# Counting edges in shorter pieces over narrower windows, in a two-layer graph kernel

## The reference, cut to what matters

```python
e = leaky_relu(a1[src] + a2[dst]); m = segment_max(e, dst)
w = exp(e - m[dst]); alpha = w / segment_sum(w, dst)
out = segment_sum(alpha[:, :, None] * ft[src], dst)      # ft = projection of x
```

## Time and profile before

| | |
|---|---|
| median of three runs | 1255.27 us (1253.35 to 1255.71) |
| profiled execution | 1256.27 us, its span 1254.6 us |
| PE busy | 1107.9 us, 88% of the span, 8043 matmuls |
| DVE busy | 1034.4 us, 82%, 1739 instructions |
| ACT busy | 653.2 us, 52%, 1080 instructions |
| POOL busy | 159.5 us, 13% |
| DMA | 98.95 MB, mean 79 GB/s |
| mean granted clock of PE | 0.968 of full speed |

### The profile page before, as it was taken

The page is one execution under the profiler, slowest core; times in us unless marked ns, Lnnn a source line. Parts: engine busy times, 40 slices in busy tenths (PEclk is TensorE's granted clock), DMA queues, the critical chain, the costliest instruction groups (busy, mean ns, idle before and its releaser), DMA issues.

```text
span 1254.6 us, 21108 instructions
## 1 busy us (share of the span) xinstructions
PE 1107.9 (88%) x8043; PEld 921.8 (73%) x8043; DVE 1034.4 (82%) x1739; ACT 653.2 (52%) x1080; POOL 159.5 (13%) x155
## 2 busy tenths in 40 slices
PE   4787865888888888869999999999979999999996
PEld 1344454666666666659999989999968888788885
DVE  7987469999999999979488589999988765267865
ACT  0322497999999999932211046667731221223432
POOL 3000000000000000000005402111430105330111
PEclk9998876999999999989999999999989999999998
DMA  3001112202020211155403641020314112435121
GB/s 133 1 13 51 52 55 82 71 13 83 1 83 2 83 34 56 37 186 171 132 25 120 229 144 42 2 75 1 135 47 156 36 51 102 154 113 204 63 73 47
DMA packets 39859, 98.95 MB, mean 79 GB/s; under 512 B 4467, under 2 KB 17147, under 8 KB 39765
## 3 DMA queue, kind: packets, MB, share of 16 engines
q1 hardware_dynamic: 39766, 97.66, 22.8%
HBM read 70.74 MB, written 26.90 MB: 78 GB/s over the span
## 4 chain that ended last, share of the span: by engine, by line
PE 42%; DVE 36%; issue 14%; ACT 3%; DVEq 2%; DMA 1%; POOL 0%; SPq 0%; POOLq 0%; ACTq 0%
DVE R L1493 14%; PE psum L967 13%; PE psum L884 12%; PE psum L995 8%; DVE R L1623 5%; DVE R L1633 5%; DVE R L1481 4%; PE psum L784 3%; DVE LC L1356 1%; PE psum L684 1%; DVE et_lo L1650 1%; PE psum L948 1%; DVE LC L1357 1%; ACT LC L1101 1%; PE psum L978 1%
## 5 line engine op out<-in xcount | busy, mean ns | idle before, releaser
L825 PE MATMUL psum<-ident,R 128*128 128x128 f32 (+3 forms) x1200 | 158.1, 280 | 52.8 <-ACT R L1116 52.2
L825 PEld LDWEIGHTS psum<-ident,R 128*128 128x128 f32 (+3 forms) x1200 | 128.2, 142 | 94.9 <-ACT R L1116 82.1
L1493 DVE CUSTOM_DVE_ANT_0 R<-R,LC 128x1250 f32<-128x1250 f32 x120 | 176.0, 1467 | 0.0
L1116 ACT ACTIVATE R<-R,row_max 128x1250 f32<-128x1250 f32 x120 | 161.0, 1342 | 7.3 <-DVE row_max L1493 4.7
L839 PE MATMUL psum<-R 128*64 128x256 f32 (+3 forms) x1200 | 146.0, 382 | 0.0
L1132 ACT COPY R<-psum 128x1280 f32<-128x1280 f32 x120 | 142.8, 1190 | 0.3 <-PE psum L825 0.3
L884 PE MATMUL psum<-w_hi,x1T_hi 128*128 128x256 f32 (+1 forms) x480 | 136.3, 284 | 3.3 <-issue 1.6
L884 PE MATMUL psum<-w_lo,x1T_hi 128*128 128x256 f32 (+1 forms) x480 | 135.2, 282 | 0.0
L884 PE MATMUL psum<-w_hi,x1T_lo 128*128 128x256 f32 (+1 forms) x480 | 135.0, 281 | 0.0
L1928 POOL TENSOR_TENSOR rstd<-rstd,minus_half 128x1 f32<-128x1 f32 (+1 forms) x40 | 32.0, 800 | 763.3 <-DVE rstd L1506 763.3
L1481 DVE SCALAR_TENSOR_TENSOR R<-R 128x1250 f32<-128x1250 f32 x80 | 122.4, 1531 | 1.1 <-DMA R<-rows_spill 1.1
(11 more groups left out here) (220 smaller groups left out, 2666.1 us busy)
## 6 DMA issues: line engine op xcount, KB each, us to landing
R<-rows_spill SPq DMA_DIRECT2D x20, 625.0 KB, 5.2
rowbuf<-rows_spill SPq DMA_DIRECT2D x14, 625.0 KB, 5.2
lc_spill<-LC SPq DMA_DIRECT2D x9, 625.0 KB
LC<-lc_spill SPq DMA_DIRECT2D x9, 625.0 KB, 6.4
res_spill<-colbuf SPq DMA_DIRECT2D x36, 128.0 KB, 2.6
R<-res_spill SPq DMA_DIRECT2D x9, 512.0 KB, 3.5
R<-in_x_dram SPq DMA_DIRECT2D x1, 3456.0 KB
res_spill<-R SPq DMA_DIRECT2D x9, 384.0 KB
```

The costliest lines, as they stand in the source:

```text
L825: last = e.transpose(turn0[r % 2][0:m, s, 0:n_dst], ring[0:n_dst, r % RING0, s * P:s * P + m], ident[0:n_dst, 0:n_dst])
L1116: e.activation(ring[0:m, r % RING0, :], ring[0:m, r % RING0, :], ACT.Exp, bias=row_max[0:m, r % RING:r % RING + 1], scale=-1.0, accum_out= ...
L1493: e.tensor_tensor_reduce(slot, slot, LC[0:m, i, :], 1.0, MIN_CEILING, ALU.add, ALU.min, row_max[0:m, r % RING:r % RING + 1]).then_inc(S.le ...
```

## The change

`WIN` goes from 64 to 48. Ten source tiles x 48 destinations are 480 columns, and these go into one PSUM bank (0 for even groups, 4 for odd ones) by one matmul for each tile; the one-hot `hot_cell` and the window that DVE adds shrink with it. A segment is no longer two groups but a part of one: three tiles or two, by turns, so that there are 68. Eight segments come first (four groups, before: six). The rest is spread by a formula: up to 18 segments by the end of the transposes of x, then 46 over the 60 units of the projection, each tested ahead of a unit, and the last ones around the transposes of the attention rows. The program of DVE keeps its order.

```diff
--- before.py
+++ after.py
@@ -51,9 +51,9 @@
     RING = 8
     GT = 5
     GROUPS = ET // GT
-    WIN = 64
+    WIN = 48
     HT = NT // 2
-    assert GROUPS * GT == ET and GROUPS % 2 == 0 and NT % 2 == 0 and HT * WIN <= BANK
+    assert GROUPS * GT == ET and GROUPS % 2 == 0 and NT % 2 == 0 and NT * WIN <= BANK
 
     x1_dram = nc.dram_tensor("x1_spill", (N, D), F32, kind="Internal").ap()
     base_dram = nc.dram_tensor("base_spill", (N, D), F32, kind="Internal").ap()
@@ -437,7 +437,7 @@
             return places
 
         def window_psum(half):
-            return psum[:, 4 * half:4 * half + 2, 0:HT * WIN].rearrange("p b (i w) -> p b i w", w=WIN)
+            return banks[4 * half][:, 0:NT * WIN].rearrange("p (i w) -> p i w", w=WIN)
 
         all_sum = [[banks[0], banks[1], banks[2]], [banks[4], banks[5], banks[6]]]
         PREP_EDGES_F, PREP_MAX, PREP_CLIP, PREP_ENDS = 4, 7, 8, 9
@@ -672,19 +672,13 @@
                 e.wait_ge(S.y_out[b], 16 * len(range(b, NT, 4)))
 
 
-        def windows_pe(e, g):
-            b = g % 2
-            halves_ = [psum[:, 4 * b + k, 0:HT * WIN] for k in range(2)]
-            if g >= 2:
+        def windows_pe(e, g, tiles):
+            if g >= 2 and tiles[0] == 0:
                 e.wait_ge(S.win_added, g - 1)
-            for j in range(GT):
-                t = g * GT + j
-                e.wait_ge(S.win_hot, t + 1)
-                for half in range(2):
-                    last = e.matmul(halves_[half], hot_row[j],
-                                    hot_cell[j][:, half * HT * WIN:(half + 1) * HT * WIN],
-                                    start=(j == 0), stop=(j == GT - 1))
-                last.then_inc(S.win_free, 1)
+            for j in tiles:
+                e.wait_ge(S.win_hot, g * GT + j + 1)
+                e.matmul(banks[4 * (g % 2)][:, 0:NT * WIN], hot_row[j], hot_cell[j], start=(j == 0),
+                         stop=(j == GT - 1)).then_inc(S.win_free, 1)
 
         def all_pe(e):
             def product(buf, g, start, stop):
@@ -709,6 +703,8 @@
                         e.wait_ge(S.all_hot, r * 2 + (g * ET + buf + 1))
                         product(buf, g, False, False).then_inc(S.all_free, 1)
                 product(None, g, False, True).then_inc(S.all_sum, 1)
+
+        FIRST_COUNTS, TURN_COUNTS, LAST_COUNTS = 8, 18, 4
 
         def pe_program(e):
 
@@ -727,17 +723,23 @@
             span = e.value_load(base_i[0:1, GROUPS:GROUPS + 1], min_val=0, max_val=N)
             e.sem_inc(S.all_free, 2)
 
+            SEGMENTS = [range(0, 3), range(3, GT)]
+            COUNTS = len(SEGMENTS) * GROUPS
+
             def count_segment(n):
+                g, part = divmod(n, len(SEGMENTS))
                 with e.If(span < WIN):
-                    windows_pe(e, 2 * n)
-                    windows_pe(e, 2 * n + 1)
-                if n == GROUPS // 2 - 1:
+                    windows_pe(e, g, SEGMENTS[part])
+                if n == COUNTS - 1:
                     with e.Else():
                         all_pe(e)
 
-            for n in range(3):
-                count_segment(n)
-            done = 3
+            def count_until(done, n):
+                for at in range(done, n):
+                    count_segment(at)
+                return max(done, n)
+
+            done = count_until(0, FIRST_COUNTS)
 
 
             e.wait_ge(S.w_in, 6 * 16)
@@ -756,9 +758,7 @@
             use = 2
             for k in range(KT):
                 for piece, (c, w) in enumerate(pieces):
-                    if piece == 0:
-                        count_segment(done)
-                        done += 1
+                    done = count_until(done, FIRST_COUNTS + (use - 2) * (TURN_COUNTS - FIRST_COUNTS) // (KT * NP))
                     if use == 2:
                         e.wait_ge(S.rhs_w, 1)
                     elif use == 3:
@@ -774,19 +774,19 @@
             e.wait_ge(S.xT, KT * NP)
             for i in range(NT):
                 m = rows[i]
-                if done < GROUPS // 2:
-                    count_segment(done)
-                    done += 1
                 for k in range(KT):
                     at = i * KT + k
+                    done = count_until(done, TURN_COUNTS + at * (COUNTS - LAST_COUNTS - TURN_COUNTS) // (NT * KT))
                     if at >= 2:
                         e.wait_ge(S.ft, at - 1)
                     e.matmul(side_bank(use)[0:m, 0:2 * P + 4], xT[:, k, i * P:i * P + m], rhs[:, k, :],
                              start=True, stop=True).then_inc(S.ft_sum, 1)
                     use += 1
+            done = count_until(done, COUNTS - LAST_COUNTS + 1)
             e.wait_ge(S.ft, NT * KT)
             for piece, (c, w) in enumerate(pieces):
                 if piece >= 2:
+                    done = count_until(done, COUNTS - 1)
                     e.wait_ge(S.rowsT, 2 * (piece - 1))
                 for i in tiles_of(piece):
                     m = rows[i]
@@ -794,9 +794,7 @@
                                        ident[0:m, 0:m])
                 last.then_inc(S.rows_turned, 1)
                 use += 1
-            while done < GROUPS // 2:
-                count_segment(done)
-                done += 1
+            count_until(done, COUNTS)
 
 
             e.wait_ge(S.counted, 1)
@@ -1360,7 +1358,7 @@
             def add(g, half):
                 e.wait_ge(S.win_free, g * GT + GT)
                 base = e.value_load(base_i[0:1, bass.ds(g, 1)], min_val=0, max_val=N - WIN)
-                window_ = CT[:, :, bass.ds(base, WIN)].rearrange("p (b i) w -> p b i w", b=2)
+                window_ = CT[:, :, bass.ds(base, WIN)]
                 e.wait_ge(S.win_added, g)
                 e.tensor_tensor(window_, window_, window_psum(half), ALU.add).then_inc(S.win_added, 1)
```

## The result

The new kernel takes 1225.09 us, median of four runs (1223.14 to 1227.60), against 1254.81 for the kernel before; the ratio is 0.9765, 95% interval 0.9743 to 0.9788. The forecast was 1214, with a range of 1208 to 1225: the direction was right, the gain is 30 us where 41 were named, and the time lies a hair outside the range. The profiled execution took 1223.14, its span 1221.4. One execution of an experiment (e10) took 1822.77 us at a granted clock of 0.559 where the others of it had 0.93 to 0.97; the ratios leave it out.

The account below looks back on a forecast made before the run. DVE was taken to pace counting, with PE's order holding it during projection. Groups of 2.775 us, a 5 us start stall and the end put the counts' transposes at 119.3 instead of 160.83: 41.5 us gained, 1214 us, range 1208 to 1225.

Parts of the forecast that it names:

- the 36.8 us behind them: From the first transpose of the counts to the rows' landing: expected to stay 36.8 us and move as a whole.
- the stalls of 13.2 us: DVE's seven waits for PE to free one-hot buffers during projection, 13.2 us in the kernel before; expected to go.
- forecast 54.7 against 61.1: Projection stretch: 54.7 us of PE work against 61.1 us for 22 groups on DVE, so DVE sets the pace.
- rival 1: PE's clock decides the projection: at a mean of 0.83, 54.7 us becomes 65.9, total 1220; chance 20%.
- nor 3: Third rival: PE stays at 1.2 GHz through the whole projection, 105 us, total 1260, slower than before; chance 3%.
- rival 2: Each counting piece costs PE 0.3 us in the projection: 68.5 us against 61.1, total 1222; chance 10%.
- the end: After the last one-hot: addition 1.3 us later, counted at 118.2, ACT's widening 0.8, semaphore 0.1, counts' transposes at 119.3.
- New group: 3.147 - 5 x 0.041 - 0.167 = 2.775 us: DVE's time for a counting group: mean 3.147 us less savings on five one-hot pairs and one addition.
- what is late next is DVE itself: Projection stretch: the 13.2 + 5.2 + 1.3 us of stalls go, then DVE itself is late next.
- I take 5 us, bounds 3 and 8: Start, around turning the weights: DVE stalls 3.4 us, plus a later addition with exposed load, taken as 5 us.
- The bounds of the group's cost (2.74 to 2.94): DVE's group time in us, if the addition's saving were 0.205 (proportional cost) or nothing (fixed cost).
- The prediction's own sign of being wrong: DVE's waits for PE between 50 and 115 us exceeding 3 us, or later stages taking other times than before.

Follow-up runs that it names:

- e10: The kernel before with only DVE's counting loop written out, windows still 64: 1251.21 us, ratio 0.9992 to the kernel before.
- e11: The new kernel with a branch of its own for each of the 170 tiles on PE, 102 more: 1222.89 us, ratio 0.9764 to the kernel before.
- e1: The kernel before, its order kept, with windows of 48 and one matmul a tile: 1252.16 us, ratio 0.9995 to the kernel before.
- e2: The new kernel's order with windows of 64, two banks and two matmuls a tile: 1230.23 us, ratio 0.9827 to the kernel before.
- e5: The new kernel with DVE's counting loop written out, only the window's base from a register: 1216.75 us, ratio 0.9717 to the kernel before.
- e6: The new kernel with four groups in a turn of DVE's loop in place of two: 1221.56 us, ratio 0.9767 to the kernel before.
- e9: The kernel before with windows of 48, one matmul a tile and DVE's loop written out: 1239.03 us, ratio 0.9882 to the kernel before.
- e8: The new kernel measured again without edit: 1223.19 us, ratio 0.9777 to the kernel before.
- e4: The new kernel with weights turned behind the fourth segment of counting, not the eighth: 1217.18 us, ratio 0.9721 to the kernel before.
- e7: The new kernel with DVE's loop written out and weights turned behind the fourth segment: 1211.37 us, ratio 0.9672 to the kernel before.
- e3: The new kernel with DVE loading the window's base ahead of the group's first tile: 1222.25 us, ratio 0.9767 to the kernel before.

## Why the prediction was wrong

**Right.** What bound the kernel; that the gain is what the counts' transposes gain, with the 36.8 us behind them unchanged; the projection's stretch, where the stalls of 13.2 us went and PE had room (busy for 54 of 62 us, forecast 54.7 against 61.1); the durations (one-hots 340 ns in the page, additions 0.65 to 0.66); PE at full clock there (rival 1 did not happen, nor 3); the branches at nothing (rival 2, e11); the end (the last addition 1.5 late for 1.3, then 1.7 to the transposes for 1.9). The Trainium skill has about 108 ns for a compare-and-branch (Advanced Engine Details and Errata, "Control Flow Timing"); by that, 5.0 in all would have stayed under cover too, but PE's idle time in e11, the same with 102 branches more, does not show it.

**Wrong, first: "New group: 3.147 - 5 x 0.041 - 0.167 = 2.775 us".** From the sixth addition (42.39) to the last but one (124.10) 27 groups took 81.71 us, 3.026 each: 6.8 us in all more than forecast. The step averaged eight groups before and took all of the 0.12 beyond the engine's work (3.03 with the loop written out, e10) for a constant. The earlier trace rows gave only the ends of that stretch; its groups were 3.11 and 3.16 apart by turns. The two are different things: the shorter one follows DVE's own work and shrank to 2.79, the longer one is the loop's edge and stayed at 3.15, whatever the width (e1, e2, the new kernel). 13 edges, each 0.375 over 2.775, are 4.9 us. The other 2 are four groups longer still (3.44, 3.64, 3.07, 3.67) and the 0.02 by which 2.79 is over 2.775; what lengthens these four is not shown, and e5 has three smaller ones. e5, e6 and e9 show that it is the edge. The statement of "what is late next is DVE itself" was right of the engine and wrong of what in it: by these runs the stream of instructions, with its registers, branch and load, and not the arithmetic.

**Wrong, second: "I take 5 us, bounds 3 and 8".** DVE stalled 4.64 + 2.06, 6.7 and within the bounds, and the additions around them were late by 0.26, 0.50 and 0.41; the sixth addition came 2.6 us later than the step gives. PE waited for ACT as forecast (3.30), but turned the first eight blocks in 1.94 us where they took 1.04 before, and three counting tiles took 1.41 for 0.78 later: the lower level of its clock, 1.2 GHz (the granted clock reads 0.50 from 28 to 38 us), after a stretch with PE mostly idle. The working priced this stretch at full clock. In e8 PE's next six transposes are back at 0.80 us, where they took 1.44 in the first profile, and the stall at the fifth addition is 0.9 shorter. e4 takes the stall of 4.64 away; its first eight transposes still take 1.91, so the clock is not what gives the 6 us.

6.8 + 2.6 = 9.4 is the 9.5 missing. In e7 the edges and the first stall are gone, and the transposes come at 115.56, 3.7 ahead of the forecast. This agrees roughly with the rows: 34 groups at 2.70 for 2.775 are 2.5 us, a stall of 2.0 for 5 is 3.0, and the longer groups that are left take some 2 back.

**The range.** It ended at 1225, from the rivals' prices. The bounds of the group's cost (2.74 to 2.94) did not hold 3.03, as they covered only the addition's price and not the engine's feeding. The same kernel measured again (e8, 1223.19) lies inside, but not because the mechanism was right: its groups come 3.15 and 2.79 apart as well, and none of the rivals that widened the range happened. The prediction's own sign of being wrong, over 3 us of DVE waiting for PE between 50 and 115, did not show either; the profile names no such wait there, and the 5.6 us lost are put down to "issue". A slip of the working: the end's terms (118.2, 0.8 and 0.1) add up to 119.1, not 119.3.

**Left open.** Whether it is the branch, the register arithmetic at the turn's start or the load behind them that makes up 3.15: moving the load only moved the wait (e3), and I took none of the others away alone. That the instruction stream is what takes the time is argued from the runs: the long group comes with the loop's edge (e5, e6), is the same for 480 and 640 columns (e2), and follows no wait that the profile names.

## What to carry to other kernels

When instructions of a looped program get shorter, look at single periods and not at their mean: a period that stays as it was for two sizes of the work points at the loop and its instruction stream, and the saving falls on the others only. Here a wait put down to "issue", which moved to another instruction and another releaser when a load was moved (e3), was of that kind; writing the loop out tested it in one run. And a change that moves work out of a gap (here counting beside ACT's 28 copies) has to be checked for what the gap's other side then waits for.

## What was not expected of the hardware

- DVE's loop edge: 3.15 to 3.16 us for a group with 2.70 us of constant-addressed work (3.03 with 640 columns); waits and addresses from registers cost 0.10 a group (2.80 against 2.70), the edge 0.36 more.
- Leaving a segment past the other program's code (the last one carries it) cost PE 3.19 us in e1 and 3.37 in e9, idle by "issue", but nothing in the kernel before, where the projection goes on at 143.62, nor in e10 (141.00). The two that stall have one matmul a tile, the two that don't have two. In the new kernel such a stall would fall beside DVE's last addition and not be seen. The Trainium skill has a rule that would fit (Runtime: NRT & Kernel Launch, "Instruction fetch mechanics"): a taken branch to a target outside the fetched window waits for a fetch. No run here tests it; the two stalls and the two absences are all that is shown.
- The clock's column does not always show a slow stretch: in e8 it gives 1.00 for 17 to 50 us, in the new kernel's first profile 0.79, and the first eight transposes of x take 1.94 us in both (1.04 before).
